# Maxima of the scores from four of six products, two heads at a time on the two halves of the array's rows

## The chip, the cores and the metric

The kernel runs on one core of one Trainium2 chip. The metric is the device time of one execution in microseconds, lower is better; a version's time is the median of its runs.

## The reference

The input is x, 4 sequences of 1024 tokens with 256 features. Four layers follow one another, each added to x after a layer norm of its input: causal attention with a latent key, a small recurrent network over features (called ffn), a gated delta-rule layer, and the ffn once more. The change touches only the attention:

```
c_kv = x @ W_dkv.T                                  # 128 latent features
q    = x @ W_dq.T @ W_uq.T                          # 16 heads of 16
q_lat = einsum('bqhd,hdl->bhql', q, k_eff)
attn = softmax(causal(einsum('bhql,bkl->bhqk', q_lat, c_kv) / sqrt(16)))
y    = einsum(attn @ c_kv, v_eff)                   # joined to x
```

The kernel folds k_eff into the keys, so that a head's score is a product of 16 features of q and 16 of k.

## The kernel before

**Split operands.** q and k are each written as a sum of three bf16 parts, high, middle and low. Six of the nine cross products are kept (`SPLIT`), laid out one under the other: a stack of 6 x 16 = 96 rows. So one bf16 matmul with 96 rows of contraction gives a score of nearly fp32 precision. `q_stack` and `k_stack` hold such stacks for four heads and 1024 tokens; there are three of each (`STACKS`). The parts go through DRAM: SP writes them out (L439) and loads the stacks from there, 12 DMAs for one unit (`load`, L431). Three more rows, 96 to 98, hold the negated maxima in three parts on the side of q, and ones on the side of k, so that the product with 99 rows is the score less its row's maximum, ready for the exponential.

**Units.** A unit is one sequence and four heads; there are 16. For a unit the maxima come first: `pairs` lists the products (block of 128 queries, bank of up to 512 keys, width, heads); there are 38, each fills a PSUM bank as far as it goes: one head at 512 or 384 columns, two at 256, four at 128. TensorE makes each (L538) after a mask product where it touches the diagonal (L534), VectorE reduces it (L739). When all are there, VectorE combines them (L744), TensorE transposes them (`negmax`, L546), VectorE splits them into three parts (L751 to L760) and SP copies each part into its row of `q_stack` (L447).

**Steps.** Then come 12 steps for the unit, one block of 128 keys against a chunk of queries each: scores (mask L603, product L607) into three banks, the exponential by ScalarE (L694), and the values (L624, fp32, four heads on four column tiles of 17), one step later. A unit's maxima are made while the unit before it is in its steps: `order` spreads them over the steps, 38 per 12 steps, with a lead of one unit and 8 (`LEAD`). `mixed` interleaves them with the scores of the same step, by equal fractions. So the order of each engine is written out by hand. The maxima use a ring of four banks (`RING`), and an item waits for the release of the one four before it.

**Prologue.** Before the first step, the first two sequences' parts are made (`project` of groups 0 to 3) between the maxima of the first unit, and the stacks of the first three units are loaded. VectorE's program starts with the rows of ones (L777), one memset for each of three stacks, and goes on to the layer norm.

Semaphores connect the engines: `unmet` gives the waits that an instruction still needs. SP runs the loads, the sends of parts and the copies of the maxima in one queue, in the order of the items.

Of the kernel before, what the change touches and what calls it, by code (L numbers as in the profile page):

```python
# [14 lines left out]
P = 128  # L15
# [10 lines left out]
HPU = 4  # L26
# [227 lines left out]
class Attention:  # L254
# [3 lines left out]

    WEIGHTS = (("wdqT", [P, KT, P]), ("wdkvT", [P, KT, P]), ("wuqT", [P, C]), ("wuq", [P, KT, P]),
# [4 lines left out]
    PRODUCTS, ROWS, MAX_ROWS = 6, 6 * HS, 3  # L264
# [4 lines left out]
    def __init__(self, k):  # L269
# [48 lines left out]
    def order(self):  # L318
# [24 lines left out]
        for i in range(lead):  # L343
            self.prologue += take(i + 1) + more[i * len(more) // lead:(i + 1) * len(more) // lead]
# [13 lines left out]
        for n, (u, kb, qc) in enumerate(self.steps):  # L358
            self.during[n] += take(lead + -(-per * (n + 1) // len(self.unit_steps)))
# [57 lines left out]
    def sync(self, e, unmet):  # L417
        k, s, io = self.k, self.s, self.k.io

        def load(u, halves):  # L420
# [4 lines left out]
            for n in range(len(self.SPLIT[0])):  # L425
                for which, dst in ((0, self.qst[st]), (1, self.kst[st])):
# [4 lines left out]
                    e.dma_start(dst[n * HS:(n + 1) * HS, :, cols], src).then_inc(*s[f"stack_in{st}"].did(u, halves[-1], n, which))  # L431

        def send(item):
# [7 lines left out]
            if item[0] == "negmax":  # L441
                u = item[1]
                for r in range(self.MAX_ROWS):
                    row = self.ROWS + r
                    for w in unmet(s["max_hi"](u), s["max_mid"](u), s["max_lo"](u), self.stack_free(u)):
                        e.wait_ge(*w)
                    e.dma_start(self.qst[u % STACKS][row:row + 1, :, :].rearrange("o h (q t) -> o (h q) t", q=QB),  # L447
                                self.mparts[u % 2][:, r, :]).then_inc(*s[f"max_in{u % STACKS}"].did(u, r))
# [64 lines left out]
    def tensor(self, e, unmet):  # L513
        k, s, bank, w_ = self.k, self.s, self.k.bank, self.w

        def stacked(u, half):
            return s[f"stack_in{u % STACKS}"](u, half if u == 0 else 1, self.PRODUCTS - 1, 1)

        def make(item):
            kind, a = item[0], item[1:]  # L520
            if kind == "norm":
                return
            out = bank[self.bank[item]]
            for w in unmet(self.released[item]):
                e.wait_ge(*w)
            if kind == "max":
                u, w_at = a
                qb, c, width, heads = self.pairs[w_at]
                st, k0 = u % STACKS, c * BANK
                diagonal = k0 + width == (qb + 1) * P  # L530
                for w in unmet(stacked(u, qb * P // BANK), k.s["const16"]("mask")):
                    e.wait_ge(*w)
                if diagonal:
                    e.matmul(out[:, 0:len(heads) * width].rearrange("p (h x) -> p h x", h=len(heads))[:, :, width - P:width],  # L534
                             k.ident16[:, :], k.mask16[:, :].rearrange("p (o x) -> p o x", o=1).to_broadcast([P, len(heads), P]),
                             start=True, stop=False, skip_group_check=True)
                for i, h in enumerate(heads):
                    m = e.matmul(out[:, i * width:(i + 1) * width], self.qst[st][0:self.ROWS, h, qb * P:(qb + 1) * P],  # L538
                                 self.kst[st][0:self.ROWS, h, k0:k0 + width], start=not diagonal and i == 0, stop=True,
                                 skip_group_check=True)  # L540
                m.then_inc(*s["max_mm"].did(u, w_at))
# [54 lines left out]
        def scores(n, i):  # L596
# [3 lines left out]
            for w in unmet(stacked(u, qc), s[f"max_in{st}"](u, self.MAX_ROWS - 1), s["k_ones"](st), self.score_free[n, i]):  # L600
# [5 lines left out]
            for j, h in enumerate(heads):  # L606
                m = e.matmul(out[:, j * width:(j + 1) * width],  # L607
                             self.kst[st][0:self.ROWS + self.MAX_ROWS, h, kb * P:(kb + 1) * P],
# [1106 lines left out]
```

## Time and profile before

| | |
|---|---|
| median of 3 runs | 1454.43 us (1452.35 to 1455.84) |
| the profiled execution | 1452.64 us |
| its span, first to last instruction | 1450.8 us |
| TensorE busy | 1218.1 us (84%) |
| VectorE busy | 880.1 us (61%) |
| ScalarE busy | 610.2 us (42%) |
| GpSimd busy | 447.5 us (31%) |
| mean granted TensorE clock | 0.92 |

The attention takes the first 650 us or so of the span. Its steps begin at 112 us and take about 31 to 36 us per unit. In the rows, PE is TensorE's matmuls, PEld its weight loads, DVE VectorE, ACT ScalarE, POOL GpSimd, SPq SP's queue. An end of a matmul in the rows is modelled, so the distance from start to start is what I go by.

### The profile page before, as it was taken

How to read it: one execution, taken by the hardware profiler on the slowest of the kernel's cores; microseconds unless marked ns; L12 is line 12 of the kernel's file. 1: busy time of each engine (PE TensorE's matmuls, PEld its weight loads, DVE VectorE, ACT ScalarE, POOL GpSimd, SP SyncE). 2: the span in 40 equal slices, each digit the busy share in tenths (PEclk: the TensorE clock that was granted, in tenths of full speed). 3: DMA queues.
4: the chain of work that ended last, by engine and by line, in shares of the span. 5: the costliest groups of instructions: out<-in, count | busy, mean ns of one | idle time of the engine just before them, and what ended most of it. 6: DMA issues, size and time to landing. Idle time of an engine off the chain costs nothing. (4 is left out here: it accounts for less than half of the span.)

```text
span 1450.8 us, 32359 instructions
## 1 busy us (share of the span) xinstructions
PE 1218.1 (84%) x13530; PEld 755.3 (52%) x13530; DVE 880.1 (61%) x1900; ACT 610.2 (42%) x1207; POOL 447.5 (31%) x663
## 2 busy tenths in 40 slices
PE   3779999999999999989999346566987858699993
PEld 1434444444444444337888323245665647488882
DVE  4466767676788777715434755677867362354346
ACT  1426666666666766655222322122332212142222
POOL 2420505142200000014231556443663313342304
PEclk7889999999999999999999768778999979899996
DMA  5492535344455333000000000011111100000003
GB/s 153 131 148 90 89 45 89 56 78 67 73 63 62 49 45 45 2 1 1 1 0 1 17 17 10 21 32 29 33 29 32 35 25 12 2 1 0 1 1 116
DMA packets 78754, 61.66 MB, mean 43 GB/s; under 512 B 41360, under 2 KB 65552, under 8 KB 78480
## 3 DMA queue, kind: packets, MB, share of 16 engines
q1 hardware_dynamic: 77456, 57.18, 21.9%
q10 hardware_dynamic: 1152, 2.41, 0.5%
q8 instruction: 106, 1.74, 0.5%
q14 instruction: 40, 0.33, 0.1%
HBM read 38.20 MB, written 20.97 MB: 41 GB/s over the span
## 5 line engine op out<-in xcount | busy, mean ns | idle before, releaser
L694 ACT ACTIVATE weights<-psum 128x512 f32<-128x512 f32 (+1 forms) x608 | 322.4, 585 | 159.4 <-PE psum L607 157.5
L739 DVE TENSOR_REDUCE maxima<-psum 128x1 f32<-128x512 f32 (+3 forms) x432 | 262.2, 662 | 57.4 <-PE psum L538 56.3
L607 PE MATMUL psum<-q_stack,k_stack 99*128 99x512 bf16 (+3 forms) x768 | 223.7, 328 | 1.3 <-ACT weights L694 1.1
L538 PE MATMUL psum<-k_stack,q_stack 96*128 96x512 bf16 (+3 forms) x768 | 213.0, 328 | 5.8 <-DMA k_stack<-qk_parts 4.1
L624 PE MATMUL psum<-weights,v_rows 128*17 128x512 f32 (+3 forms) x1536 | 162.0, 494 | 0.1
L510 POOL TENSOR_TENSOR residual<-residual,att_o 128x256 f32<-128x256 f32 x32 | 23.2, 725 | 364.0 <-DVE att_o L772 364.0
L900 PE MATMUL psum<-f_xT,f_weights_hi 128*128 128x512 f32 x384 | 123.5, 403 | 0.0
L739 DVE TENSOR_REDUCE negmax<-psum 128x1 f32<-128x384 f32 (+3 forms) x176 | 102.3, 634 | 27.8 <-PE psum L538 26.2
L607 PEld LDWEIGHTS psum<-q_stack,k_stack 99*128 99x128 bf16 x768 | 72.5, 98 | 83.1 <-ACT weights L694 38.6
L965 ACT ACTIVATE f_gates<-psum,ffn_biases 128x512 f32<-128x512 f32 x72 | 49.7, 690 | 155.8 <-PE psum L906 155.8
L1335 PE MATMUL psum<-d_w_qkb,d_hT 128*128 128x260 f32 x128 | 48.0, 510 | 68.3 <-DVE d_attnT_k_kb_v L1505 57.8
L538 PEld LDWEIGHTS psum<-k_stack,q_stack 96*128 96x128 bf16 x768 | 72.4, 99 | 56.9 <-issue 7.9
L906 PE MATMUL psum<-f_state_parts,f_weights_hi 128*128 128x512 f32 x288 | 90.4, 395 | 0.0
L603 PE MATMUL psum<-identity,mask_scores 128*128 128x128 bf16 (+2 forms) x352 | 87.1, 248 | 3.7 <-DMA q_stack<-max_parts 2.7
L534 PE MATMUL psum<-mask_scores,identity 128*128 128x128 bf16 (+2 forms) x352 | 86.7, 246 | 2.3 <-DVE a_rest L730 1.2
L603 PEld LDWEIGHTS psum<-identity,mask_scores 128*128 128x128 bf16 x352 | 34.0, 97 | 96.1 <-ACT weights L694 58.3
L900 PEld LDWEIGHTS psum<-f_xT,f_weights_hi 128*128 128x128 f32 x384 | 71.8, 191 | 16.2
L900 PE MATMUL psum<-f_xT,f_weights_lo 128*128 128x512 f32 x192 | 76.4, 398 | 0.0
L1340 PE MATMUL psum<-d_w_vg,d_hT 128*128 128x512 f32 x128 | 75.7, 724 | 0.0
L1335 PEld LDWEIGHTS psum<-d_w_qkb,d_hT 128*128 128x128 f32 x128 | 27.6, 239 | 77.0 <-DVE d_attnT_k_kb_v L1505 42.7
L1056 DVE COPY f_hidden<-psum 128x512 f32<-128x512 f32 x16 | 11.0, 690 | 91.4 <-PE psum L918 91.4
L906 PEld LDWEIGHTS psum<-f_state_parts,f_weights_hi 128*128 128x128 f32 x288 | 54.1, 188 | 13.3
(165 smaller groups left out, 2277.9 us busy)
## 6 DMA issues: line engine op xcount, KB each, us to landing
qk_parts<-a_parts SPq DMA_DIRECT2D x32, 384.0 KB, 3.6
q_stack<-qk_parts SPq DMA_DIRECT2D x90, 128.0 KB, 7.1
k_stack<-qk_parts SPq DMA_DIRECT2D x90, 128.0 KB, 7.8
residual<-in_x SPq DMA_DIRECT2D x8, 512.0 KB, 7.5
out_x<-residual SPq DMA_DIRECT2D x8, 512.0 KB, 3.8
ffn_weights<-in_ffn_w ACTq DMA_DIRECT2D x1, 2048.0 KB, 9.1
systems<-d_a_rows SPq DMA_DIRECT2D x32, 64.0 KB, 1.8
d_systems<-systems SPq DMA_DIRECT2D x4, 512.0 KB, 4.8
```

What stands on the lines that cost most here:

```text
L534: e.matmul(out[:, 0:len(heads) * width].rearrange("p (h x) -> p h x", h=len(heads))[:, :, width - P:width], k.ident16[:, :], k.mask16[:, : ...
L538: m = e.matmul(out[:, i * width:(i + 1) * width], self.qst[st][0:self.ROWS, h, qb * P:(qb + 1) * P], self.kst[st][0:self.ROWS, h, k0:k0 + ...
L603: e.matmul(out[:, 0:len(heads) * width].rearrange("p (h x) -> p h x", h=len(heads))[:, :, 0:P], k.mask16[:, :], k.ident16[:, :].rearrange( ...
L607: m = e.matmul(out[:, j * width:(j + 1) * width], self.kst[st][0:self.ROWS + self.MAX_ROWS, h, kb * P:(kb + 1) * P], self.qst[st][0:self.R ...
L624: m = e.matmul(bank[7][32 * h:32 * h + HS + 1, off:off + width], self.v_rows[:, b * QB + kb, g * HPU + h, :], self.weights[n % 2][:, h, 0: ...
L694: e.activation(self.weights[n % 2][:, heads[0]:heads[-1] + 1, 0:width], bank[self.score_bank[n, i]][:, 0:len(heads) * width].rearrange("p ...
L739: e.tensor_reduce(to, bank[self.bank[item]][:, 0:len(heads) * width].rearrange("p (h x) -> p h x", h=len(heads)), AXIS_X, ALU.max, negate= ...
L900: m = e.matmul(bank[bk][:, :], w_hi_lo[wp][:, gate, kt, ms], x[:, v, kt, :], start=q == 0, stop=t == 0 and q == len(self.TERMS) - 1)
L906: m = e.matmul(bank[bk][:, :], w_hi_lo[wp][:, 4 + gate, kt, ms], self.state_parts[j][:, v, kt, :], start=False, stop=q == len(self.TERMS) - 1)
L965: e.activation(gs[:, gate, mt, :], next_bank()[:, :], func, bias=(k.ffn_b if t else self.bias0)[:, gate, mt:mt + 1]).then_inc(*s["gate"].d ...
L1335: m = e.matmul(qk_bank[:, 0:NQ + DH], cols[kt], self.w_qkb[:, kt, :], start=kt == 0, stop=kt == KT - 1)
L1340: m = e.matmul(vg_bank[:, :], cols[kt], self.w_vg[:, kt, :], start=kt == 0, stop=kt == KT - 1)
```

## The change

The maxima are computed from the first four products of the stack alone (64 rows), in place of all six; the scores, and so the weights, still from six. The four heads of a unit are two halves. Heads 0 and 1 keep their rows: products in 0 to 95, maxima in 96 to 98. Heads 2 and 3 have their first four products in rows 64 to 127, the other two in 32 to 63, the maxima in rows 0 to 2, and rows 3 to 31 are zero on the side of q. A product of a maximum for one of the first two heads uses rows 0 to 63 of the array, one for one of the last two rows 64 to 127, and the two are issued one behind the other, to two banks. The scores use 99 rows for heads 0 and 1 and 128 for heads 2 and 3.

With this, the maxima come in pairs of items: 40 per unit in place of 38, two heads at most in one bank, and both items of a pair are issued at the place of the first, after the release of both banks. Each DMA into a stack is split in two, one for each half of the heads, and so is each copy of the maxima. VectorE has three memsets per stack. The essential lines:

```diff
+    HALVES = (range(0, HPU // 2), range(HPU // 2, HPU))
+    ROW = (tuple(n * HS for n in range(6)), (64, 80, 96, 112, 32, 48))
+    MAX_ROW, LEADING, ALL_ROWS = (96, 0), (slice(0, 64), slice(64, P)), (slice(0, 99), slice(0, P))
...
-                n = min(HPU, BANK // width)
-                self.pairs += [(qb, c, width, range(h, h + n)) for h in range(0, HPU, n)]
+                n = min(HPU // 2, BANK // width)
+                self.pairs += [(qb, c, width, range(half[h], half[h] + n)) for h in range(0, HPU // 2, n) for half in self.HALVES]
...
-            self.prologue += take(i + 1) + more[i * len(more) // lead:(i + 1) * len(more) // lead]
+            self.prologue += take((i + 2) // 2 * 2) + more[i * len(more) // lead:(i + 1) * len(more) // lead]
...
-            self.during[n] += take(lead + -(-per * (n + 1) // len(self.unit_steps)))
+            self.during[n] += take(lead + -(-per * (n + 1) // (2 * len(self.unit_steps))) * 2)
...
-                    e.dma_start(dst[n * HS:(n + 1) * HS, :, cols], src).then_inc(*s[f"stack_in{st}"].did(u, halves[-1], n, which))
+                    for side, heads in enumerate(self.HALVES):
+                        row, hs_ = self.ROW[side][n], slice(heads[0], heads[-1] + 1)
+                        e.dma_start(dst[row:row + HS, hs_, cols], src[:, hs_, :]
+                                    ).then_inc(*s[f"stack_in{st}"].did(u, halves[-1], n, which, side))
...
+                    for side, heads in enumerate(self.HALVES):
+                        row, hs_ = self.MAX_ROW[side] + r, slice(heads[0], heads[-1] + 1)
+                        e.dma_start(self.qst[u % STACKS][row:row + 1, hs_, :].rearrange("o h (q t) -> o (h q) t", q=QB),
+                                    self.mparts[u % 2][heads[0] * QB:(heads[-1] + 1) * QB, r, :]
+                                    ).then_inc(*s[f"max_in{u % STACKS}"].did(u, r, side))
...
+        def maximum(u, w_at):
+            if w_at % 2:
+                return
...
+            for w in unmet(*[self.released[item] for item in both], stacked(u, qb * P // BANK), k.s["const16"]("mask")):
+                e.wait_ge(*w)
+            for out in outs if diagonal else ():
+                e.matmul(out[:, 0:len(heads) * width].rearrange("p (h x) -> p h x", h=len(heads))[:, :, width - P:width],
+                         k.ident16[:, :], k.mask16[:, :].rearrange("p (o x) -> p o x", o=1).to_broadcast([P, len(heads), P]),
+                         start=True, stop=False, skip_group_check=True)
+            for i in range(len(heads)):
+                for side, out in enumerate(outs):
+                    h, rows = self.pairs[w_at + side][3][i], self.LEADING[side]
+                    m = e.matmul(out[:, i * width:(i + 1) * width], self.qst[st][rows, h, qb * P:(qb + 1) * P],
+                                 self.kst[st][rows, h, k0:k0 + width], start=not diagonal and i == 0, stop=True,
+                                 skip_group_check=True)
+                    if i == len(heads) - 1:
+                        m.then_inc(*s["max_mm"].did(u, w_at + side))
...
-            e.memset(self.kst[st][self.ROWS:self.ROWS + self.MAX_ROWS, :, :], 1.0).then_inc(*s["k_ones"].did(st))
+            low, high = slice(0, HPU // 2), slice(HPU // 2, HPU)
+            e.memset(self.kst[st][96:99, low, :], 1.0).then_inc(*s["k_ones"].did(st, "low"))
+            e.memset(self.kst[st][0:32, high, :], 1.0).then_inc(*s["k_ones"].did(st, "high"))
+            e.memset(self.qst[st][0:32, high, :], 0.0).then_inc(*s["k_ones"].did(st))
```

## Rows read from the trace of the kernel before

**Rows 1.** busy by stretch: us, PE, PEld, DVE, ACT, POOL busy, clock, DMA, GB/s

```profile
450.00:550.00 100.00, 99.77 (x792) 43.80 (x789) 79.54 (x151) 67.19 (x128) 4.35 (x6) 1.00 0.40 49
```

**Rows 2.** the page's costliest groups: busy, mean ns, idle before and its releaser

```profile
L607 PE MATMUL psum<-q_stack,k_stack 99*128 99x512 bf16 (+3 forms) x768 | 223.7, 328 | 1.3 <-ACT weights L694 1.1
L538 PE MATMUL psum<-k_stack,q_stack 96*128 96x512 bf16 (+3 forms) x768 | 213.0, 328 | 5.8 <-DMA k_stack<-qk_parts 4.1
```

**Rows 3.** timeline, TensorE, steady stretch: start us, us, engine, line, operation, count

```profile
409.36 0.38 PE L538 MATMUL psum<-k_stack,q_stack 96*128 96x512 bf16 x1
...
409.57 0.38 PE L607 MATMUL psum<-q_stack,k_stack 99*128 99x512 bf16 x1
...
409.88 0.41 PE L624 MATMUL psum<-weights,v_rows 128*17 128x128 f32 x8
...
410.23 0.39 PE L607 MATMUL psum<-q_stack,k_stack 99*128 99x512 bf16 x1
```

**Rows 4.** timeline, TensorE, the later layer with 32x32 tiles

```profile
1108.68 1.88 PE L1340 MATMUL psum<-d_w_vg,d_hT 128*128 128x512 f32 x4
1110.49 0.65 PE L1349 MATMUL psum<-d_qT_kT_kbT 32*32 32x64 f32 x32
1110.96 0.62 PE L1358 MATMUL psum<-d_attnT_k_kb_v,d_w_u 32*32 32x64 f32 x32
```

**Rows 5.** copies of maxima (min/median/max ns); timelines of units 1 and 8

```profile
L447 SPq DMA_DIRECT2D q_stack<-max_parts x48: 503/584/1347, 107.7 to 615.2; - x48
...
DMA to landing us min/median/max: 1.7/1.8/3.6
...
142.42 1.78 SPq L447 DMA_DIRECT2D q_stack<-max_parts  x3
...
147.47 0.23 PE L603 MATMUL psum<-identity,mask_scores 128*128 128x128 bf16 x1
...
394.86 1.78 SPq L447 DMA_DIRECT2D q_stack<-max_parts  x3
...
398.18 0.10 PEld L603 LDWEIGHTS psum<-identity,mask_scores 128*128 128x128 bf16 x1 [0.42 <-DMA q_stack<-max_parts]
```

**Rows 6.** timeline, end of the maxima of unit 8

```profile
391.19 0.38 PE L538 MATMUL psum<-k_stack,q_stack 96*128 96x512 bf16 x1
...
391.61 0.69 DVE L739 TENSOR_REDUCE maxima<-psum 128x1 f32<-128x512 f32 x1 [1.08 <-PE psum L538]
...
392.34 0.17 DVE L744 TENSOR_TENSOR negmax<-maxima 128x16 f32<-128x16 f32 x1
...
392.86 0.27 PE L546 MATMUL psum<-identity,negmax 128*32 128x128 f32 x1
```

**Rows 7.** timeline, VectorE at the start: first two memsets, first layer norm

```profile
10.04 3.47 DVE L777 MEMSET k_stack<- 3x4096 bf16 x1 [0.91 <-issue]
14.31 3.47 DVE L777 MEMSET k_stack<- 3x4096 bf16 x1 [0.80 <-issue]
...
22.68 0.75 DVE L221 BATCH_NORM_STATS2 ln_stats<-residual 128x6 f32<-128x256 f32 x2
```

**Rows 8.** SP timeline, SP waits, busy by stretch, ScalarE timeline

```profile
65.71 0.32 SPq L431 DMA_DIRECT2D q_stack<-qk_parts  x1
...
82.27 0.43 SPq L431 DMA_DIRECT2D k_stack<-qk_parts  x1
...
SPq L438 <- POOL a_parts L496: 151.2, 25, 28.1
...
65.70:71.20 5.50, 5.03 (x18) 2.04 (x16) 3.13 (x6) 1.63 (x3) 1.22 (x3) 1.00 0.49 104
71.20:82.70 11.50, 7.90 (x28) 4.08 (x29) 6.77 (x11) 3.73 (x7) 3.12 (x3) 0.85 1.07 128
82.70:101.00 18.30, 14.52 (x59) 6.79 (x56) 12.24 (x27) 3.99 (x7) 5.14 (x9) 0.91 1.08 147
...
101.29 0.60 ACT L679 ACTIVATE a_parts<-psum 128x512 bf16<-128x512 f32 x1 [5.20 <-DMA qk_parts<-a_parts]
```

More of the change, by code:

```diff
@@ L263 @@
     SPLIT = ((0, 1, 0, 1, 2, 0), (0, 0, 1, 1, 0, 2))
-    PRODUCTS, ROWS, MAX_ROWS = 6, 6 * HS, 3
+    PRODUCTS, MAX_ROWS = 6, 3
+    HALVES = (range(0, HPU // 2), range(HPU // 2, HPU))
+    ROW = (tuple(n * HS for n in range(6)), (64, 80, 96, 112, 32, 48))
+    MAX_ROW, LEADING, ALL_ROWS = (96, 0), (slice(0, 64), slice(64, P)), (slice(0, 99), slice(0, P))
     LEAD = 8
@@ L516, in stacked @@
         def stacked(u, half):
-            return s[f"stack_in{u % STACKS}"](u, half if u == 0 else 1, self.PRODUCTS - 1, 1)
+            return s[f"stack_in{u % STACKS}"](u, half if u == 0 else 1, self.PRODUCTS - 1, 1, 1)
+        def maximum(u, w_at):
+            if w_at % 2:
+                return
+            qb, c, width, heads = self.pairs[w_at]
+            st, k0, both = u % STACKS, c * BANK, [("max", u, w_at), ("max", u, w_at + 1)]
+            outs, diagonal = [bank[self.bank[item]] for item in both], k0 + width == (qb + 1) * P
+            for w in unmet(*[self.released[item] for item in both], stacked(u, qb * P // BANK), k.s["const16"]("mask")):
[12 more added lines that the diff above has]
+                        m.then_inc(*s["max_mm"].did(u, w_at + side))
         def make(item):
@@ L522, in make @@
                 return
+            if kind == "max":
+                maximum(*a)
+                return
             out = bank[self.bank[item]]
@@ L525, in make @@
                 e.wait_ge(*w)
[L526 to L541, printed above, removed]
             if kind == "negmax":
@@ L599, in scores @@
             q0, width = self.span(n)
-            for w in unmet(stacked(u, qc), s[f"max_in{st}"](u, self.MAX_ROWS - 1), s["k_ones"](st), self.score_free[n, i]):
+            for w in unmet(stacked(u, qc), s[f"max_in{st}"](u, self.MAX_ROWS - 1, 1), s["k_ones"](st), self.score_free[n, i]):
                 e.wait_ge(*w)
@@ L606, in scores @@
             for j, h in enumerate(heads):
-                m = e.matmul(out[:, j * width:(j + 1) * width],
-                             self.kst[st][0:self.ROWS + self.MAX_ROWS, h, kb * P:(kb + 1) * P],
-                             self.qst[st][0:self.ROWS + self.MAX_ROWS, h, q0:q0 + width],
+                rows = self.ALL_ROWS[h in self.HALVES[1]]
+                m = e.matmul(out[:, j * width:(j + 1) * width], self.kst[st][rows, h, kb * P:(kb + 1) * P],
+                             self.qst[st][rows, h, q0:q0 + width],
                              start=not self.diagonal(n) and j == 0, stop=True, skip_group_check=True)
@@ L748, in take @@
                 rows, n = bank[self.bank[item]][0:HPU * QB, 0:P], u % 2
-                for w in unmet(s["negmax_T"](u), s[f"max_in{(u - 2) % STACKS}"](u - 2, self.MAX_ROWS - 1) if u >= 2 else None):
+                for w in unmet(s["negmax_T"](u), s[f"max_in{(u - 2) % STACKS}"](u - 2, self.MAX_ROWS - 1, 1) if u >= 2 else None):
                     e.wait_ge(*w)
```

5 lines of the change are left out of this document (1 added, 4 removed).

## The prediction, made before the change was run

> **What bounds the kernel now.** I read four views in this order. The busy times by stretch come first: in a hundred microseconds in the middle of the attention TensorE is busy throughout at the full granted clock, VectorE for 80 and ScalarE for 67 of them [rows 1]. So TensorE's order of work sets the time there, if its matmuls really stream back to back. The grouped instructions say what it does: the maxima's products (L538), the scores (L607) and the values (L624) [rows 2]. The timeline then shows how close they stand: 512 columns of L607 follow 512 columns of L538 after 0.21 to 0.22 us, which is the 2.4 GHz level with nothing between, and the height of the operand (96, 99 or 128 rows) makes no difference [rows 3]. Last I looked for places where TensorE waits for others: at the start of a unit [rows 5], and in the first hundred microseconds [rows 7, 8]. There the order of SP and VectorE counts, not TensorE's columns.
>
> The sum is made against the profiled execution: 1452.6 us, span 1450.8. That stands 1.8 us under the median of 1454.4, which I add at the end.
>
> **TensorE: columns saved, array modes paid for.** Per unit the maxima stream 4 heads x 36 blocks of 128 = 18432 columns, 7.7 us at 2.4 GHz, 123 us over 16 units. With two heads side by side half of it goes: 3.84 us per unit. That presumes that two row halves overlap. The nearest rows are the 32x32 tiles of the later layer: 32 matmuls of 64 fp32 columns take 0.47 us, where one alone would need about 0.054 (half of the 0.108 us that a 128-column fp32 pass takes in its stream), 1.7 us in a row. They run nearly four at a time [rows 4]. But these write different partitions, while the two halves here write the same partitions in two banks; no row shows that.
>
> What it costs is the change of shape of the array. A value group (17-column tiles, L624) starts 0.31 us after a 512-column product, so 0.09 late, and the product after its 128 columns comes 0.35 us after it, where two passes of 128 columns need 0.21 to 0.22: 0.13 late [rows 3]. Going to 32x32 tiles costs the same: four passes of 512 fp32 columns would take 1.71 us, the tiles come after 1.81 [rows 4]. I take 0.20 to 0.22 us for a visit. No row shows a change to two halves of 64 rows, so its bounds are 0 and 0.22; I take the upper end, since both kinds of tile that the trace has pay it. Number of visits: I wrote out TensorE's order of one unit by the change's rules. 40 maxima are 20 pairs, and the scores stand between nearly all of them. The mask matmul ahead of 12 of the 20 uses the whole array too. Today there are about 23 changes of shape per unit (12 value groups), after it 58: 35 more at 0.10, plus some 17 first loads at 0.02 that nothing covers, 3.8 us per unit. It eats the 3.84 us. TensorE's own change is 0, between -3.8 and 0 us per unit for the switches alone.
>
> The Trainium skill bears on this, "TensorEngine Tiling (Array Packing)", Key Properties: changing the tiling mode, not just the tile, drains the engine. The trace agrees for the modes that it has, with 0.09 to 0.13 us per change; for 64-row halves it has none. By that rule the gain is gone, and without it some 55 us are saved.
>
> Two more maxima per unit and the two extra mask matmuls add no columns. VectorE gets 40 reductions in place of 38 over the same elements; it has 20 us in 100 free [rows 1], so they are hidden.
>
> **The start of a unit: three more issues on SP.** Scores wait for the three rows of maxima that SP copies into the stack (L447). One such DMA takes 0.58 us to issue, three take 1.78, so the next follows after 0.60 to 0.62; each lands 1.8 to 1.85 us after its issue [rows 5]. In unit 8 the three are issued from 394.86, the third at 396.06, it lands at 397.9 and the scores start at 398.18: 0.25 us to spare. The change issues six, with half the elements each. I price the three at the same 0.62, since issue times here hardly depend on size (0.43 us for 128 KB of stack, 0.58 for 8 KB [rows 5, 8]): 1.87 us; the cheapest single issue, 0.32 [rows 8], is the lower bound, 1.0 us. I read the same two rows for all units. The spare time is 1.5 us in unit 0, 2.0 in unit 1 [rows 5], 0.2 to 1.1 in the next ten, and none in the last four, which already wait. Subtracting it unit by unit leaves 21.5 us (9 us at the lower bound). What is queued on TensorE behind these scores is everything: the maxima of the next unit and the values.
>
> **The reduction ahead of the transpose.** Step 9 of a unit holds the last maxima, then the negmax transpose (L546). Today the last product stands at 391.19, its reduction ends at 392.30, the combination starts at 392.34, and the transpose at 392.86 follows the matmul before it without a gap [rows 6]. After the change the last two maxima arrive together and VectorE needs two reductions of 0.64: 0.42 until the first can start, 1.28, then 0.21 and some 0.1 of signal, 2.0 us after the pair. TensorE gets there in about 1.5 us of work. So it waits 0.45 us, 15 times: 7 us, between 0 (were the ring of banks early enough) and 15. It is not hidden by the wait above, because the six DMAs start only behind this transpose.
>
> The pair also waits for both of its banks, which of the ring of four is the release of the third item before it, where one maximum waits for the fourth. VectorE needs 1.3 us for a pair and the pairs come at 1.1 to 1.3 us, two pairs deep; I count nothing, at most 0.5 us per unit.
>
> **Startup.** VectorE fills the rows of ones before it touches the first tokens. Three memsets of 4096 elements start 4.27 us apart (their rows say 3.47 busy; start to start counts) and only then, at 22.68, comes the layer norm [rows 7], for which everyone waits. The change has nine memsets of 2048: 9 x 2.14 = 19.2 against 12.8 us, 6.4 us later. Nothing covers it. A bound below is 2.1 us if only the ones were paid, none above 6.4.
>
> The stack loads double in number: 12 issues at a pitch of 0.467 us become 24, each half as large [rows 8]. The first half load is delayed by 5.6 us but meets slack, for the sends behind it wait for GpSimd. The second begins at 65.71 and is followed by 24 loads of whole stacks; the DMA engines are half busy until 71.2 and saturated from there [rows 8], until the next sends land and ScalarE, which waits for them, goes on at 101.29 [rows 8]. With 12 more issues of 0.467 the saturated part begins 5.6 us later. The 48 issues that follow take 22.4 us where the data needs over 26, so they stay behind the data. I take 5.6 us; bounds 0 (idle DMA time elsewhere takes it in) and 11 (the first delay counts too). Later loads (11 us of issue in a unit of 31) are ready long before they are used.
>
> **Sum.** 6.4 + 5.6 + 21.5 + 7 + 0 = 40.5. 1452.6 + 40.5 = 1493.1 for the execution, 1495 on the median; the terms with a floor below lean down, so I say 1493.
>
> **Rivals.**
> A, the forecast: halves overlap, switches cost as other tiles do, SP and startup decide. The terms' own bounds give 1470 to 1518. Chance 0.70.
> B, ends faster: the change of shape between the whole array and its halves is free. For it speaks that operands of 96, 99 and 128 rows mix without cost [rows 3]; against it, both other tile shapes. TensorE then saves 35 x 0.10 + 0.3 = 3.8 us per unit, 61 us; some 12 to 15 us of it are given back, as about three pairs lie between the transpose and the next scores, where the six DMAs are awaited. 1493 - 47 = 1446. It turns faster than before once a change of shape costs less than about 0.01 to 0.02 us. Chance 0.14.
> C, the halves don't overlap (same partitions, two banks): the columns aren't saved, 61 us more, 1554. For it speaks only that no row shows that case; against it, four tiles at once in the later layer [rows 4]. Chance 0.06. The Trainium skill, "TensorE: Matmul & The Clock Gate", Part 3, gives 3.07 times the speed for four row tiles of 512 columns; by that C would not happen, and no run here has shown it.
> D, the small costs are mostly hidden: issues at the lower bound (-12.5), no startup loss for the loads (-5.6), no wait before the transpose (-7). 1468. Chance 0.10.
>
> **Chances and range.** 1446 to 1518 takes in A's range, D, and the upper half of B; it leaves out C and the rest of B. About 0.2% (3 us) is what a measurement can tell from none: faster 0.13 (B without its upper edge), same 0.04, slower 0.83 (A, C, D).
>
> **What would show each step.** In the profile after: the layer norm's first VectorE row near 29.1 and not 22.7; ScalarE's release by the sends near 113; x6 issues of L447's successor over about 3.7 us, and TensorE idle 1.5 to 2 us before each unit's first scores; start to start from a 512-column whole-array product to a half pair about 0.31 us, out of it about 0.33; the two halves of a pair some 10 ns apart. If pair entry shows 0.22 us, B is right; if halves stand 0.21 us apart, C is. If the six issues come at a pitch of 0.35, the unit starts lose only half. The whole is wrong if the time is below 1446.

## The result, and the profile after

The changed kernel takes 1489.0 us (median of 4 runs, 1486.68 to 1494.15), the kernel before 1454.07 (4 runs on the same chip, 1452.35 to 1455.84). The ratio is 1.0245, with a 95% interval of 1.0215 to 1.0275. The profiled execution took 1488.27 us with a span of 1486.4, at a mean granted clock of 0.92, as before. The forecast was 1493.

**Stretch.** The busy times of a hundred microseconds in the attention (columns as in [rows 1]):

```profile
450.00:550.00 100.00, 92.35 (x736) 33.19 (x741) 74.75 (x148) 62.80 (x120) 4.36 (x6) 1.00 0.18 49
```

TensorE was busy for all 100 us in [rows 1] and is now idle for 7.65 of them, at the same full clock. The DMA engines' busy share fell from 0.40 to 0.18 at the same 49 GB/s, which nothing in the prediction says.

**Groups.** From the page of the changed kernel, the products of scores, the products of maxima, the masks ahead of the scores, and the loads of the stacks:

```profile
L626 PE MATMUL psum<-q_stack,k_stack 99*128 99x512 bf16 (+5 forms) x720 | 197.7, 327 | 4.7 <-ACT weights L712 4.6
L544 PE MATMUL psum<-k_stack,q_stack 64*128 64x512 bf16 (+3 forms) x768 | 116.8, 336 | 14.0 <-DMA k_stack<-qk_parts 8.7
L621 PE MATMUL psum<-identity,mask_scores 128*128 128x128 bf16 (+2 forms) x352 | 88.7, 252 | 18.5 <-DMA q_stack<-max_parts 16.8
...
q_stack<-qk_parts SPq DMA_DIRECT2D x180, 64.0 KB, 2.3
k_stack<-qk_parts SPq DMA_DIRECT2D x180, 64.0 KB, 2.3
```

The same rows of the kernel before, for the masks and the loads:

```profile
L603 PE MATMUL psum<-identity,mask_scores 128*128 128x128 bf16 (+2 forms) x352 | 87.1, 248 | 3.7 <-DMA q_stack<-max_parts 2.7
...
q_stack<-qk_parts SPq DMA_DIRECT2D x90, 128.0 KB, 7.1
k_stack<-qk_parts SPq DMA_DIRECT2D x90, 128.0 KB, 7.8
```

The 768 products of maxima keep TensorE busy for 116.8 us where they took 213.0 [rows 2]. So the halves do overlap. The masks ahead of a unit's first scores now wait 16.8 us for the copies of the maxima, where they waited 2.7. The last number of a load's row is the time from its issue to its landing: 2.3 us in place of 7.1 and 7.8. (48 of the 768 scores have no record in this trace.)

**Steady order.** The timeline of TensorE in one step (columns as in [rows 3]):

```profile
441.56 0.38 PE L626 MATMUL psum<-q_stack,k_stack 99*128 99x512 bf16 x1
441.79 0.28 PE L538 MATMUL psum<-mask_scores,identity 128*128 128x128 bf16 x2
441.99 0.39 PE L544 MATMUL psum<-k_stack,q_stack 64*128 64x512 bf16 x2
442.31 0.23 PE L621 MATMUL psum<-identity,mask_scores 128*128 128x128 bf16 x1
442.38 0.38 PE L626 MATMUL psum<-q_stack,k_stack 99*128 99x512 bf16 x1
442.60 0.22 PE L621 MATMUL psum<-identity,mask_scores 128*128 128x128 bf16 x1
442.66 0.38 PE L626 MATMUL psum<-q_stack,k_stack 128*128 128x512 bf16 x1
442.88 0.22 PE L621 MATMUL psum<-identity,mask_scores 128*128 128x128 bf16 x1
```

Two masks of 128 columns need 0.11 us of stream; the pair starts 0.20 after them, so 0.09 late. The two halves of the pair share one row: two products of 512 columns with one start (3 ns apart). What follows starts 0.32 us after them, where one product's columns need 0.213: 0.10 late. Whole-array operands of 99 and of 128 rows both release the next matmul after 0.22 us (442.38 to 442.60, 442.66 to 442.88).

**Where the 35.6 us of span come from.** The first scores of unit 0 start at 121.87 in place of 112.31 (+9.6), those of unit 15 at 653.42 in place of 617.05 (+36.4), and the rest of the program gives 0.8 back. So there are two places: the prologue, and 26.8 us in the units. From one unit's first scores to the next, units 9 and 10, which no work for a later sequence disturbs, take 33.4 and 33.5 us in place of 31.06. (Units are counted from 0.)

**Prologue.** VectorE at the start, after:

```profile
9.25 1.76 DVE L796 MEMSET k_stack<- 3x2048 bf16 x1 [0.48 <-issue]
11.50 1.76 DVE L797 MEMSET k_stack<- 32x2048 bf16 x1 [0.48 <-issue]
13.42 0.91 DVE L798 MEMSET q_stack<- 32x1024 uint32 x1 [0.16 <-issue]
14.82 1.76 DVE L796 MEMSET k_stack<- 3x2048 bf16 x1 [0.48 <-issue]
...
25.97 1.33 DVE L221 BATCH_NORM_STATS2 ln_stats<-residual 128x6 f32<-128x256 f32 x4
```

The layer norm is 3.3 us later than in [rows 7]. Then the timeline of SP and ScalarE around the loads of whole stacks, after:

```profile
72.36 0.79 SPq L437 DMA_DIRECT2D q_stack<-qk_parts  x2
...
105.62 0.89 SPq L437 DMA_DIRECT2D k_stack<-qk_parts  x2
106.62 2.83 SPq L446 DMA_DIRECT2D qk_parts<-a_parts  x4
...
109.41 0.60 ACT L697 ACTIVATE a_parts<-psum 128x512 bf16<-128x512 f32 x1 [2.13 <-DMA qk_parts<-a_parts]
```

And the busy times of two stretches of it (the last two columns are the DMA share and GB/s):

```profile
88.00:100.00 12.00, 9.87 (x46) 4.26 (x44) 10.83 (x25) 5.84 (x10) 3.90 (x5) 0.86 0.52 137
100.00:112.00 12.00, 10.00 (x34) 3.52 (x34) 8.12 (x15) 2.90 (x5) 3.68 (x7) 0.85 0.71 215
```

SP issues 72 loads without a pause at 0.467 us and comes to the next sends only at 106.62. Before, they were issued from 82.81 on and then stood behind the data, with a DMA share above 1 [rows 8]. Now the DMA engines are half idle (0.52), so it is SP's issues that take the time, not the data.

**A unit.** The end of the maxima of unit 9, the copies, and its first scores, after:

```profile
446.69 0.27 PE L564 MATMUL psum<-identity,negmax 128*32 128x128 f32 x1 [0.33 <-DVE negmax L762]
...
448.40 3.67 SPq L455 DMA_DIRECT2D q_stack<-max_parts  x6
...
451.37 0.63 PE L642 MATMUL psum<-weights,v_rows 128*17 128x256 f32 x8
...
453.23 0.23 PE L621 MATMUL psum<-identity,mask_scores 128*128 128x128 bf16 x1 [1.24 <-DMA q_stack<-max_parts]
```

The transpose waits for VectorE's combination; the six copies take 3.67 us of SP; the scores wait until the last of them has landed, 1.24 us of idle time. From start to start: the value group at 451.37 needs 0.56, and the scores come after 1.86.

### The profile page after: what moved, and what is told of

Same layout as the page of the kernel before. It is cut to its first block and busy times, and to the rows that moved or that the text cites. A ratio compares the mean times of both kernels' runs of the same rounds, so it can differ in the third digit from the quotient of the medians.

```text
span 1486.4 us, 32738 instructions
## 1 busy us (share of the span) xinstructions
PE 1220.5 (82%) x13514; PEld 719.7 (48%) x13562; DVE 885.5 (60%) x1938; ACT 613.0 (41%) x1207; POOL 448.1 (30%) x663
## 3 DMA queue, kind: packets, MB, share of 16 engines
q1 hardware_dynamic: 81488, 57.20, 13.5%
## 5 line engine op out<-in xcount | busy, mean ns | idle before, releaser
L712 ACT ACTIVATE weights<-psum 128x512 f32<-128x512 f32 (+1 forms) x608 | 325.7, 581 | 183.0 <-PE psum L626 180.8
L757 DVE TENSOR_REDUCE maxima<-psum 128x1 f32<-128x512 f32 (+2 forms) x448 | 261.7, 645 | 75.1 <-PE psum L544 74.8
L626 PE MATMUL psum<-q_stack,k_stack 99*128 99x512 bf16 (+5 forms) x720 | 197.7, 327 | 4.7 <-ACT weights L712 4.6
L757 DVE TENSOR_REDUCE negmax<-psum 128x2 f32<-128x256 f32 (+2 forms) x192 | 103.5, 595 | 48.2 <-PE psum L544 48.2
L544 PE MATMUL psum<-k_stack,q_stack 64*128 64x512 bf16 (+3 forms) x768 | 116.8, 336 | 14.0 <-DMA k_stack<-qk_parts 8.7
L626 PEld LDWEIGHTS psum<-q_stack,k_stack 99*128 99x128 bf16 (+1 forms) x768 | 68.3, 98 | 87.6 <-ACT weights L712 50.4
L621 PE MATMUL psum<-identity,mask_scores 128*128 128x128 bf16 (+2 forms) x352 | 88.7, 252 | 18.5 <-DMA q_stack<-max_parts 16.8
L1361 PE MATMUL psum<-d_w_vg,d_hT 128*128 128x512 f32 x128 | 79.5, 755 | 0.0
L538 PE MATMUL psum<-mask_scores,identity 128*128 128x128 bf16 (+1 forms) x384 | 60.6, 239 | 9.2 <-DVE maxima L757 5.0
L544 PEld LDWEIGHTS psum<-k_stack,q_stack 64*128 64x128 bf16 x768 | 30.6, 94 | 69.0 <-issue 43.1
```

The lines of the kernel that those rows point to most:

```text
L626: m = e.matmul(out[:, j * width:(j + 1) * width], self.kst[st][rows, h, kb * P:(kb + 1) * P], self.qst[st][rows, h, q0:q0 + width], start= ...
L712: e.activation(self.weights[n % 2][:, heads[0]:heads[-1] + 1, 0:width], bank[self.score_bank[n, i]][:, 0:len(heads) * width].rearrange("p ...
L757: e.tensor_reduce(to, bank[self.bank[item]][:, 0:len(heads) * width].rearrange("p (h x) -> p h x", h=len(heads)), AXIS_X, ALU.max, negate= ...
L1361: m = e.matmul(vg_bank[:, :], cols[kt], self.w_vg[:, kt, :], start=kt == 0, stop=kt == KT - 1)
```

## The experiments

The ratios of the first four are to 1452.45 us for the kernel before (7 runs), those of the last four to 1452.05 us (15 runs). Except where it is said, each computes the same as the kernel it is made from. "Period" is the time from the first scores of unit 9 to those of unit 10.

From the first scores of unit 15 to the end, no maxima are left and the code is the same in all of these kernels; yet this stretch takes from 827.7 us (`a_whole`) to 840.0 (`b_copies6`) in their traces, 833.7 in the kernel before. So a difference of a few microseconds between two totals says less than the periods and the starts of units do.

### The order of pairs alone

`b_pairs` is the kernel before with its items in pairs (40 per unit, both issued at the first one's place, after both banks are free). The stacks, their loads and the copies are as before, and the maxima still come from all six products.

```diff
-                n = min(HPU, BANK // width)
+                n = min(HPU // 2, BANK // width)
-            self.during[n] += take(lead + -(-per * (n + 1) // len(self.unit_steps)))
+            self.during[n] += take(lead + -(-per * (n + 1) // (2 * len(self.unit_steps))) * 2)
+            for w in unmet(*[self.released[item] for item in both], stacked(u, qb * P // BANK), k.s["const16"]("mask")):
```

> The kernel before with only the order of the change: 40 maxima in pairs, both banks awaited, two heads at most in a bank; still all six products (96 rows) on the whole array, one head at a time, no split DMA, three memsets. My theory: the pairs cost only the wait ahead of the transpose, 0.33 to 0.45 us in 15 units, 5 to 7 us: 1460 us. Rival 1: the ring of banks, awaited two at a time, starves TensorE in the short steps: 15 us or more, 1469 and up. Rival 2: the order costs nothing: 1454.

Measured: 1462.21 us, ratio 1.0065 (1.0046 to 1.0084); period 31.88, 0.82 more than before. The timeline of TensorE, with one row of VectorE, in a step with two pairs, and at the transpose of unit 10:

```profile
453.85 0.60 PE L617 MATMUL psum<-q_stack,k_stack 99*128 99x512 bf16 x2
453.90 0.42 DVE L782 TENSOR_TENSOR att_o<-psum,att_rden 128x256 f32<-128x256 f32 x1
454.47 0.27 PE L530 MATMUL psum<-mask_scores,identity 128*128 128x128 bf16 x2
...
464.12 0.27 PE L556 MATMUL psum<-identity,negmax 128*32 128x128 f32 x1 [0.31 <-DVE negmax L754]
```

The transpose's bracket says 0.31 us, but ends of matmuls are modelled: from start to start the transpose comes 0.47 us later than the columns before it need. The first three rows show another cost. Two products of 512 columns need 0.43 us and the pair's masks start 0.62 after the first of them, 0.19 late. One of the pair's two banks had been free for 2 us; the other is freed by VectorE's att_o, which ends at 454.32: a pair waits for the later of its two banks. The order moved the scores together too, and once per unit a score waits 0.3 us for ScalarE. Together that is 0.47 for the transpose and 0.4 for banks (0.57 where the kernel before has 0.17). So the order of pairs costs 0.8 us per unit by itself.

### The layout alone, maxima on the whole array

`a_whole` is the changed kernel with both halves of the heads laid out in rows 0 to 98. The pairs, the split loads, the six copies and nine memsets stay. The maxima come from all six products again.

```diff
-    ROW = (tuple(n * HS for n in range(6)), (64, 80, 96, 112, 32, 48))
-    MAX_ROW, LEADING, ALL_ROWS = (96, 0), (slice(0, 64), slice(64, P)), (slice(0, 99), slice(0, P))
+    ROW = (tuple(n * HS for n in range(6)), tuple(n * HS for n in range(6)))
+    MAX_ROW, LEADING, ALL_ROWS = (96, 96), (slice(0, 64), slice(64, P)), (slice(0, 99), slice(0, 99))
-                    h, rows = self.pairs[w_at + side][3][i], self.LEADING[side]
+                    h, rows = self.pairs[w_at + side][3][i], slice(0, 96)
-            e.memset(self.kst[st][0:32, high, :], 1.0)
+            e.memset(self.kst[st][96:P, high, :], 1.0)
```

> The changed kernel with its order, its split DMAs and its nine memsets, but both halves of the heads laid out in rows 0 to 98, and the maxima from all six products on the whole array: no half rows. So 3.84 us of columns per unit come back and 35 changes of shape at 0.10 us plus the first loads that nothing covers go. My theory (the two cancel): 1489 within 6 us, and the same wait at each unit's start. Rival B (a change of shape to half rows is free): about 50 us slower than the changed kernel, 1535 and up. Rival (a change of shape costs more than the columns bring, beyond 0.12 us each): 1480 or less.

Measured: 1486.30 us, ratio 1.0235 (1.0216 to 1.0255), so within 3 us of the changed kernel. That the totals come so close is in part chance: in the traces unit 0's first scores are 3.8 us later in `a_whole` (125.66 against 121.87), and the stretch from unit 15's first scores on is 5.3 us shorter, with the same code. The units are the better measure. The period is 33.13 against 33.41, and from unit 0's first scores to unit 15's it is 530.0 us against 531.5. Doing the maxima on half the columns is worth nothing: B is refuted, and the time is lost in everything around them.

The starts of TensorE's matmuls in one such unit tell where, with the columns at 2.4 GHz taken off and the few products without a record put back (us per unit):

| | before | b_pairs | a_whole | after |
|---|---|---|---|---|
| columns of the maxima | 7.68 | 7.68 | 7.68 | 3.84 |
| late starts of values after another shape | 1.06 | 1.06 | 1.06 | 0.81 |
| into and out of half pairs | 0 | 0 | 0 | 3.80 |
| waits for banks (VectorE, ScalarE) | 0.17 | 0.57 | 0.56 | 1.02 |
| the transpose's wait | 0 | 0.46 | 0.46 | 0.48 |
| the first scores' wait for the copies | 0 | 0 | 1.25 | 1.39 |
| period | 31.06 | 31.88 | 33.13 | 33.41 |

Between the last two columns 3.84 us of columns go, 3.55 come back as changes of shape, and 0.46 because TensorE now reaches the banks before VectorE or ScalarE has freed them. There are 19 visits to the halves in a unit, 0.094 us into one and 0.10 out of it. (The table has only what differs between the four, so its columns don't add up to the period. A unit starts with its own wait for the copies, which varies: 1.30 us late for unit 9, 1.39 for unit 10.)

### Six copies of the maxima alone

`b_copies6` is the kernel before with each copy of the maxima split in two.

```diff
-                    e.dma_start(self.qst[u % STACKS][row:row + 1, :, :].rearrange("o h (q t) -> o (h q) t", q=QB),
-                                self.mparts[u % 2][:, r, :]).then_inc(*s[f"max_in{u % STACKS}"].did(u, r))
+                    for half in (0, HPU // 2):
+                        e.dma_start(self.qst[u % STACKS][row:row + 1, half:half + HPU // 2, :].rearrange("o h (q t) -> o (h q) t", q=QB),
+                                    self.mparts[u % 2][half * QB:(half + HPU // 2) * QB, r, :]
+                                    ).then_inc(*s[f"max_in{u % STACKS}"].did(u, r, half))
```

> The kernel before with only the three copies of the maxima split into six, each of half the heads; nothing else. My theory: three more issues at 0.62 us less each unit's spare time, 21 us in all: 1475 us, the issues 0.62 us apart, TensorE waiting for the copies at the start of 14 units. Rival (smaller copies issue at 0.33 us): 9 us, 1463. Rival (the stretch is covered by what TensorE still has to do): 1454 to 1457.

Measured: 1481.26 us (1475.92 to 1488.37), ratio 1.0201 (1.0163 to 1.0238), 29 us slower where 21 to 23 were expected. TensorE at the transpose of unit 10, SP, and TensorE at the unit's start, in its timeline:

```profile
466.48 0.27 PE L548 MATMUL psum<-identity,negmax 128*32 128x128 f32 x1
...
468.48 3.67 SPq L448 DMA_DIRECT2D q_stack<-max_parts  x6
...
473.38 0.23 PE L605 MATMUL psum<-identity,mask_scores 128*128 128x128 bf16 x1 [1.51 <-DMA q_stack<-max_parts]
```

From its list of waits (us in total, times, longest):

```profile
PE psum L605 <- DMA q_stack<-max_parts: 23.0, 16, 2.9
```

The wait is 23.0 us in this kernel against 2.7 in the one before: +20.3, near the 21.5 of the prediction's term. The period is 32.63, so 1.57 more: three issues of 0.62 us less the 0.28 to spare. That is not all of it. By its trace the first scores of unit 15 are 24.7 us late: units 12 and 13 last 35.6 and 34.9 us, and in units 2 and 12 to 14 one of the six issues takes 1.29 to 1.99 us itself. Another 6 us of its span stand behind unit 15's first scores, and runs of this kernel lie 12 us apart. Why some issues take so long, and what makes up the other two, stays open.

In the changed kernel the same copies cost less, 16.8 us. The pairs hide none of it: from the transpose to the first scores the kernel before takes 5.33 us and `b_pairs`, with three copies too, 5.36. But the copies start sooner there. Here SP's first issue comes 2.00 us after the transpose, since VectorE has two more reductions to do before it splits the transposed maxima; in the changed kernel it comes after 1.71 (446.69 to 448.40), and in `b_pairs` too. The rest of the difference is the long issues.

### The changed kernel with a longer lead

`a_lead12` starts the maxima of the next unit four items earlier.

```diff
-    LEAD = 8
+    LEAD = 12
```

> The changed kernel with the maxima 12 instead of 8 items ahead of the scores, so that the transpose comes about one step (2.7 us) earlier against the next unit's scores. My theory (the six issues behind the transpose are the wait at the unit starts): the 1.2 to 1.4 us of wait vanish in 15 units, about 18 us: 1471, with the wait ahead of the transpose unchanged. Rival (the wait only moves, VectorE or the banks take its place): 1484 to 1489. A little is lost in the prologue, 0 to 2 us.

Measured: 1462.29 us, ratio 1.0066 (1.005 to 1.0082), 27 us less than the changed kernel and 9 less than expected. Unit 9 in its timeline, from its last pair of maxima on:

```profile
428.69 0.39 PE L544 MATMUL psum<-k_stack,q_stack 64*128 64x512 bf16 x2
...
429.34 1.05 PE L642 MATMUL psum<-weights,v_rows 128*17 128x512 f32 x8
...
431.70 0.27 PE L564 MATMUL psum<-identity,negmax 128*32 128x128 f32 x1
...
433.25 3.67 SPq L455 DMA_DIRECT2D q_stack<-max_parts  x6
...
440.26 0.23 PE L621 MATMUL psum<-identity,mask_scores 128*128 128x128 bf16 x1
```

Neither the transpose nor the first scores wait: 8.56 us lie between them in place of 6.54, and the last copy has landed 2.2 us before it is needed. The expectation took only the scores' wait off. The transpose's went too: the items stand in the same order, but four items earlier the last pair falls at the end of one step and the transpose into the next, with a whole value group (429.34) between them. So TensorE comes to the transpose 3.0 us after that pair, not in the 1.5 us of work that the changed kernel has there, and VectorE needs 2.0. The period of 31.66 is near that of the changed kernel less both waits (33.41 - 1.39 - 0.48 = 31.54). It is 0.24 above `b_pairs` less its transpose wait (31.88 - 0.46 = 31.42), which is `a_whole`'s verdict again: half rows gain nothing over the order of pairs.

### The rows of ones written later

`b_late_ones` is the kernel before with VectorE's three memsets moved behind the first two layer norms.

```diff
-        for st in range(STACKS):
-            e.memset(self.kst[st][self.ROWS:self.ROWS + self.MAX_ROWS, :, :], 1.0).then_inc(*s["k_ones"].did(st))
-        for item in self.prologue:
+        for at, item in enumerate(self.prologue):
             take(item)
+            if at == 1:
+                for st in range(STACKS):
+                    e.memset(self.kst[st][self.ROWS:self.ROWS + self.MAX_ROWS, :, :], 1.0).then_inc(*s["k_ones"].did(st))
```

> The kernel before with its three memsets of ones moved behind the layer norm of the first two groups of tokens; nothing else. My theory (VectorE's memsets ahead of the first layer norm delay everything one for one): the first norm starts at about 10 us instead of 22.7, and the whole is 12 to 13 us shorter: 1440. Rival (tokens, weights or the DMA engines at 71 to 101 us set the end of the prologue): 0 to 6 us shorter, 1446 to 1452.

Measured: 1439.63 us (1435.41 to 1444.4), ratio 0.9911 (0.9878 to 0.9943), 12.4 us faster than the kernel before. It is the fastest of all. VectorE at its start:

```profile
9.17 1.34 DVE L221 BATCH_NORM_STATS2 ln_stats<-residual 128x6 f32<-128x256 f32 x4
...
13.27 3.47 DVE L781 MEMSET k_stack<- 3x4096 bf16 x1 [0.91 <-issue]
17.54 3.47 DVE L781 MEMSET k_stack<- 3x4096 bf16 x1 [0.80 <-issue]
```

The layer norm starts 13.5 us earlier than in [rows 7], and 12.3 of them arrive at unit 0's first scores (100.01): VectorE's time ahead of the first tokens is nearly all time of the kernel. That is the premise of the memset term, now measured.

### The split loads alone

`b_loads24` is the kernel before with each load of a stack split into heads 0, 1 and heads 2, 3, both in the old rows.

```diff
-                    e.dma_start(dst[n * HS:(n + 1) * HS, :, cols], src).then_inc(*s[f"stack_in{st}"].did(u, halves[-1], n, which))
+                    for side in range(2):
+                        hs_ = slice(side * HPU // 2, (side + 1) * HPU // 2)
+                        e.dma_start(dst[n * HS:(n + 1) * HS, hs_, cols], src[:, hs_, :]
+                                    ).then_inc(*s[f"stack_in{st}"].did(u, halves[-1], n, which, side))
```

> The kernel before with each of its loads of a stack split into two of half the heads, as in the change; copies of the maxima, order and products as before. The prediction's model (the data set the pace, and 12 more issues of 0.47 us come on top): 5.6 us, 1458 to 1460. What the trace of the changed kernel suggests instead (half loads land in 2.3 us and keep the DMA engines half as busy, so that SP's issues set the pace of the prologue): 2 to 4 us, 1455 to 1457, the DMA share in the middle about 0.2 against 0.45.

Measured: 1462.47 us (1458.66 to 1466.49), ratio 1.0066 (1.0028 to 1.0104), 10 us slower; neither size that was expected. Unit 0's first scores start at 120.07, +7.8 us, and the periods are unchanged (31.06). Its loads, from its page:

```profile
q_stack<-qk_parts SPq DMA_DIRECT2D x180, 64.0 KB, 3.8
k_stack<-qk_parts SPq DMA_DIRECT2D x180, 64.0 KB, 3.9
```

The busy times of two stretches:

```profile
72.00:108.00 36.00, 23.89 (x86) 11.19 (x85) 19.57 (x38) 8.16 (x14) 8.25 (x11) 0.81 0.82 113
450.00:550.00 100.00, 99.62 (x778) 43.09 (x775) 79.76 (x152) 68.01 (x130) 5.08 (x7) 1.00 0.35 49
```

And the timeline of SP and ScalarE at the second group's sends:

```profile
102.92 2.78 SPq L442 DMA_DIRECT2D qk_parts<-a_parts  x4
...
109.21 0.60 ACT L682 ACTIVATE a_parts<-psum 128x512 bf16<-128x512 f32 x1 [5.60 <-DMA qk_parts<-a_parts]
```

ScalarE is released at 109.21, 7.9 us after 101.29 [rows 8]. The trace's span is 13.8 us longer: 7.8 of them lie here, 0.5 in the units, and 5.6 behind unit 15's first scores, where the code is the same. So the loads delay the prologue by 7.8 us, and again SP's issues set the pace: 72 in a row, then the sends at 102.92 in place of 82.81. The split alone shortens a load's way from 7.1 to 3.8 us and lowers the DMA share a little (0.40 to 0.35). In `a_whole`, whose loads have the same size and go to the same rows as here, it is 3.4 us and 0.23; in the changed kernel, whose loads differ from those of `a_whole` only in the rows they go to, 2.3 us and 0.18. So the size of a load explains a little of the fall, and the rows in which the stacks stand another part. Between this kernel and `a_whole` neither differs, and what lowers the share there no run tells; the order of pairs alone (`b_pairs`, 0.40) and the six copies alone (`b_copies6`, 0.41) don't.

### The two repairs together

`c_lead_late` is the changed kernel with LEAD = 12 and its nine memsets behind the first two norms. The edits are those of `a_lead12` and `b_late_ones`.

> The changed kernel with a lead of 12 items and its nine memsets behind the layer norm of the first two groups. The two repairs should add up: 1462 of the lead alone, less 15 to 16 us for memsets that hold up nothing: 1447, a little under the kernel before. Rival: the late memsets collide with VectorE's first work on the parts, and half is lost: 1455.

Measured: 1450.74 us (10 runs, 1446.94 to 1452.28), ratio 0.9989 (0.9975 to 1.0003): no difference from the kernel before. The repairs add up: 27 us, then 11.6 more. The period is 31.66, and unit 0's first scores start at 107.39. `b_late_ones` with whole-array maxima is still 11 us faster. So the change is not a good idea with two mistakes around it; its core gains nothing.

### Half pairs beside the values

`c_grouped` tries to save changes of shape: `c_lead_late`, with each step's order changed to all scores, the masks of the pairs, the first pair, the values, the second pair. A pair next to the values has one change of shape where it had two.

```diff
+            if rest[:1] and rest[0][0] == "max":
+                maximum(*rest[0][1:], products=False)
+                if second:
+                    maximum(*second[1:], products=False)
+                maximum(*rest[0][1:], masks=False)
             if 0 < n <= len(self.steps):
                 values(n - 1)
+            if second:
+                maximum(*second[1:], masks=False)
```

> As the one with lead 12 and late memsets, but TensorE makes the pairs of a step next to its value group: all scores, the masks of both pairs, the first pair, the values, the second pair. Some 20 more changes of shape per unit than the kernel before in place of 35, so 15 x 0.10 = 1.5 us per unit. My theory (changes of shape are what eats the gain): 20 us less than without, 1425 to 1430. Rival (scores in one burst wait for ScalarE and the banks of the second pair for VectorE): no gain or a loss, 1447 and up.

Measured: 1470.55 us, ratio 1.0139 (1.0112 to 1.0166), 20 us slower than `c_lead_late`; the rival was right. TensorE in its timeline:

```profile
451.12 0.39 PE L626 MATMUL psum<-q_stack,k_stack 128*128 128x512 bf16 x1 [0.47 <-ACT weights L726]
451.89 0.27 PE L538 MATMUL psum<-mask_scores,identity 128*128 128x128 bf16 x2 [0.39 <-DVE maxima L771]
```

And from its list of waits:

```profile
PE psum L626 <- ACT weights L726: 16.4, 40, 0.6
```

With the scores back to back they wait for ScalarE to free one of three banks, and with the pairs back to back they wait for VectorE. The mixing that made so many changes of shape was what kept these two from being waited for.

## Why the prediction came out right, term by term

The forecast was 1493.0 for a measured 1489.0, and the case it called likeliest was the true one. Its terms were less exact than their sum: two costs of a unit were put some 7 us too high and some 13 too low, and the loads' term was near for a wrong reason. That the total came within 4 us is partly luck.

**TensorE, predicted 0.** The step had three claims. The halves overlap: right, they start 3 ns apart, and C falls. The shape costs 0.20 to 0.22 us a visit: 0.094 + 0.10 measured. It had been taken from tiles of other shapes, and the alternative, that operands of different height mix freely, concerned another thing: they all stand in the whole array. The Trainium skill, "TensorEngine Tiling (Array Packing)", Key Properties, says that a change of tiling mode drains the engine; the trace agrees for 64-row halves too, with these numbers. The savings and the cost cancel: right to 0.3 us per unit (-3.84, +3.55). What failed is the sentence "I count nothing, at most 0.5 us per unit" on the banks. That wait rose by 0.85 us per unit, 0.4 of it by the order of pairs alone. VectorE's part of it can be seen in unit 10 of the changed kernel:

```profile
496.25 0.39 PE L626 MATMUL psum<-q_stack,k_stack 99*128 99x512 bf16 x1
...
496.93 0.39 PE L538 MATMUL psum<-mask_scores,identity 128*128 128x256 bf16 x2 [0.29 <-DVE maxima L757]
```

A score of 512 columns needs 0.22 us and the next matmul comes after 0.68, 0.46 late. The reductions that free its two banks end at 496.28 and 496.88. The prediction had looked at VectorE's average, 80 of 100 us, and an average doesn't say when the second of two banks comes free.

**Start of a unit, predicted 21.5.** The mechanism is right: six issues in mostly 3.67 to 3.80 us, a pitch of 0.62 to 0.64 although each copy is half as large, and the wait in its place. `b_copies6` shows +20.3 us of waiting. In the changed kernel it is 16.8 against 2.7, so +14.1. Two readings of the kernel before didn't carry over. The copies start 1.71 us after the transpose and not 2.00, 0.29 us per unit that the subtraction didn't have. And the last four units, to which the prediction gave no spare time, wait 6.1 us in all in the changed kernel after 2.7 before, so +3.4 where it had counted 7.5.

**Ahead of the transpose, predicted 7 (0.45 x 15).** 0.33 us by the bracket, 0.49 from start to start, in 14 units: 7 us. Right, and it is the pairs that make it, as `b_pairs` has it without any half rows.

**Memsets, predicted 6.4.** 3.3. The place was right and the size wrong: nine memsets take 16.3 us and not 19.2 (9.25 to 25.57), and the first starts 0.8 us earlier than before. The three that write zeros are recorded as 1024 elements of uint32 and take 1.02 to 1.40 us from start to start where the ones take 1.92 to 2.25. The Trainium skill, "VectorE: DVE Perf Modes", "Zero memsets can be issued as uint32 (trn2)", says that a memset of zeros over 2-byte elements can be issued at 4 bytes per element, over half as many of them. The rows agree (32x1024 uint32), and the prediction had not used it. Its floor of 2.1 us "if only the ones were paid" doesn't follow from its rows either: six memsets at 2.14 are the 12.8 us of before, so the floor is 0.

**Loads, predicted 5.6.** The size is near, the reason was wrong. Unit 0's first scores are 9.6 us later. 3.3 of these are memsets and about 1 is a stretch at the lower clock, by the distances of the starts (the trace has no row of the granted clock for it): four products of L597 from 37.80 on take 2.88 us where the same four took 1.85 before, and the sends of the first parts start at 45.13, 4.24 later than before. That leaves 5.3; `b_loads24` measures 7.8 where nothing else is changed. But the failed step is "The 48 issues that follow take 22.4 us where the data needs over 26, so they stay behind the data". The data took less, the issues were the longer of the two, and the sends behind them started 23.8 us later (106.62 for 82.81). They then landed within 2.8 us and not after 18. The two errors nearly cancelled, which is luck. The prediction took the time of the data as given, though it was the change that remade the data's shape.

**Sum.** Predicted: 12.0 us in the prologue and 28.5 in the units. Measured: 9.6 and 26.8. In the units, the wait at the start came out 7 us lower, and the waits for banks (0.85 us in a steady unit, some 13 in 15 such) took its place. The sum of the terms stood at 1495 for the median; the last 2 us down to 1493 were a choice. The bounds of rival A are not those of its terms: with issues, loads, transpose and memsets at their stated floors the sum is 1464, below D's 1468 and not 1470.

**Rivals.** B needed a change of shape under 0.02 us; it is 0.10. C needed halves 0.21 us apart. D, in which the small costs were hidden, was wrong for the copies and the transpose. `a_lead12` reaches the state that D describes for these two, at 1462, but it takes another order of work.

## What to carry to other kernels

Count the visits to another array shape before counting the columns saved: at 0.2 us a visit, a pair of 512 columns saves 0.213 us and is worth it only where pairs stand together, and they can stand together only if the banks and the engines that empty them allow it. Where work is handed out in pairs, the wait is for the later of the two banks and for the second of the two reductions; look at when each comes free, not at an engine's share. Splitting a DMA in two doubled its issue time on SP's queue here, so a split costs most where the queue's issues stand ahead of something that everybody waits for; the cheapest gain of this study, 12 us, was to move three memsets from ahead of the first tokens to behind them.

## What was not expected of the hardware

- Two products on rows 0 to 63 and 64 to 127, writing the same partitions of two PSUM banks, start 3 ns apart and run side by side; 768 of them took 116.8 us of TensorE in place of 213.0.
- A change between the whole array and its halves costs 0.094 us in and 0.10 out, close to the 0.09 and 0.13 of column tiles [rows 3].
- SP's issue time of a copy of one row is the same for half the elements (median 0.589 against 0.584 us), and a stack load's is the same too (median 0.423 us at 64 KB, 0.426 at 128 KB).
- Loads of the same bytes with half the size each land after 2.3 us (here), 3.4 (`a_whole`) or 3.8 (`b_loads24`) in place of 7.1 to 7.8, with a DMA share of 0.18, 0.23 or 0.35 in place of 0.40. The rows they go to explain only the step from 0.23 to 0.18; the rest stays open.
- A memset's row shows less than its time: 3.47 us busy at 4.27 from start to start, 1.76 at 1.92 to 2.25.
